# Sampling sets of twelve tokens, with the grid distances made in SBUF from turned rows

## The chip, the cores and the metric

The kernel runs on one core of one Trainium2 chip. The metric is the device time of one execution in microseconds (us), as a median of three runs. In the profile PE is TensorE's matmuls, PEld its weight loads, DVE VectorE, ACT ScalarE, POOL GpSimd, and SPq the queue of SyncE, which issues most transfers.

## The reference, cut to what matters

Four images of 32 x 32 tokens with 128 channels each pass three layers: a deformable convolution, an attention over slices, and a mixture of eight experts. Only the sampling of the first layer changes here. Per token, with 8 groups (g) of 32 channels and 9 points (k) each:

```python
px = ww + deform[..., 0];  py = hh + deform[..., 1]
x0 = jnp.floor(px);  y0 = jnp.floor(py)
wx1 = px - x0;  wx0 = 1.0 - wx1
wy1 = py - y0;  wy0 = 1.0 - wy1
samp = gather(y0, x0) * (wy0 * wx0)[..., None] + gather(y0, x0 + 1) * (wy0 * wx1)[..., None] \
     + gather(y0 + 1, x0) * (wy1 * wx0)[..., None] + gather(y0 + 1, x0 + 1) * (wy1 * wx1)[..., None]
out = jnp.einsum('bhwgkc,bhwgk->bhwgc', samp, weights)
```

`gather` takes the value of one pixel of the group, and zero outside the image. All of it is float32.

## The kernel before, in words

**The sampling as products.** The kernel gathers nothing. The weight of pixel (y, x) for a point at (py, px) is max(0, 1 - |y - py|) * max(0, 1 - |x - px|), so one token of a group has a 32 x 32 matrix A[y, x], the sum over its nine points of an outer product, and its output is A times the group's values (`vd`). An image has 8 groups, the program 32 (`IMAGES_GROUPS`, `ig` in the code).

**Sets.** A set is what one pair of 64-row halves of TensorE's array does at once. Before, it is 8 tokens: two halves (`NI`) of `NU * NV` = 4 tokens, 36 of 64 rows. `ysb` is the stationary operand (u by 32 rows y = 64 columns), `xsb` the moving one (32 columns x by v = 64). A group has 128 sets in four batches of 32; each batch is built and used in two halves of 16 sets, so there are eight halves, called slots here, per group and 256 in the program.

**One slot** (`k = 2 * n + pair`) passes these stations: `distances` on TensorE (L770: two bf16 matmuls whose stationary operand `lp` holds the positions split in three bf16 parts, and whose moving operand `spread_b` gives each set its 32 grid points; they leave p - q in PSUM banks 4 and 5); ACT `take_x` (L1170) and `x_ramps` (L1180, two instructions) make `xsb`; DVE `take_y` (L1475) clamps the y distance into `yr`, and POOL multiplies it with the rows `rw` into `ysb` (L691, two instructions); TensorE `products` (L783, 32 matmuls, seen as 64 in the trace since each float32 one is two passes) writes one of two pairs of PSUM banks; DVE `take` (L1485) copies them to `asb`. `distances` and `take_y` run three slots ahead of the products.

**One group** ends with `contract` (L798: 128 matmuls of A with `vd`, PSUM banks 0 to 3), ACT `spread_out` (L1187), and a group later `project` (L806) and DVE `conv_add` (L1494).

**What sets the order.** Each engine has one instruction stream, written out by loops over the slots; semaphores (`s.a_summed` and so on) join them. Into each slot `side` puts pieces of other work from tables of slot numbers: the preparation of the next images' positions (`PE_PREP`, `DVE_PREP`, ...; slots of image 0 only), and for the image before, attention (slots 2 to 33), sorting tokens by expert (30 to 42), and one expert tile per slot (`TILE_SLOTS`, L1023 and L1036, two lots of 4 matmuls). After the last group a tail runs the last image's side work alone. The preparation (`find_places`, `split_places`, `edge_weights`, L1415 to L1457 on DVE) leaves the positions as bf16 parts and the weights as float32 rows; both go to DRAM and come back by DMA, group by group.

## Time and profile before

| | us |
|---|---|
| median of 3 runs (1462.43 to 1470.79) | 1466.11 |
| span of the profiled execution | 1426.0 |
| median less span (launch and end lie outside the span) | 40.1 |
| before the first product | 63.0 |
| the 32 groups, to the last product | 1149 |
| the tail | 214 |
| busy: PE, PEld | 1075.1, 864.2 |
| busy: DVE, ACT, POOL | 877.5, 755.4, 700.6 |

The profile was taken of one execution and gives no time of it beyond its span. Busy times are sums over an engine's own instructions; they overlap between engines. Two things are to be kept in mind when reading: the trace lacks about half the records of the bf16 matmuls (259 of 512, while their 512 weight loads are all there), and the ends of matmuls are modelled, so that the starts of TensorE's instructions are the firmer numbers.

### The profile page before, as it was taken

How to read it: one execution, taken by the hardware profiler on the slowest of the kernel's cores; microseconds unless marked ns; L12 is line 12 of the kernel's file. 1: busy time of each engine (PE TensorE's matmuls, PEld its weight loads, DVE VectorE, ACT ScalarE, POOL GpSimd, SP SyncE). 2: the span in 40 equal slices, each digit the busy share in tenths (PEclk: the TensorE clock that was granted, in tenths of full speed). 3: DMA queues.
4: the chain of work that ended last, by engine and by line, in shares of the span. 5: the costliest groups of instructions: out<-in, count | busy, mean ns of one | idle time of the engine just before them, and what ended most of it. 6: DMA issues, size and time to landing. Idle time of an engine off the chain costs nothing.

```text
span 1426.0 us, 63149 instructions
## 1 busy us (share of the span) xinstructions
PE 1075.1 (75%) x27983; PEld 864.2 (61%) x28236; DVE 877.5 (62%) x1579; ACT 755.4 (53%) x1444; POOL 700.6 (49%) x675
## 2 busy tenths in 40 slices
PE   3477777876886789988877789988767899785290
PEld 2365655664575568875656578865655688544290
DVE  6577768776767765566776655567886654345311
ACT  2456667665564556765643566665554565221060
POOL 6365556664442854448536644467438543211304
PEclk9689899999998899999987899999988999965595
DMA  6513141421000435521113225511013254101761
GB/s 151 146 30 63 52 104 51 109 92 35 27 28 19 115 83 160 160 79 49 33 34 104 81 82 163 146 52 45 12 49 118 71 163 141 44 15 36 228 193 57
DMA packets 166290, 121.97 MB, mean 86 GB/s; under 512 B 45642, under 2 KB 146051, under 8 KB 165507
## 3 DMA queue, kind: packets, MB, share of 16 engines
q1 hardware_dynamic: 161922, 109.53, 27.3%
q0 software_dynamic: 4096, 8.40, 2.0%
q8 instruction: 223, 3.65, 1.1%
q14 instruction: 49, 0.39, 0.1%
HBM read 89.38 MB, written 28.51 MB: 83 GB/s over the span
## 4 chain that ended last, share of the span: by engine, by line
PE 36%; DVE 16%; issue 7%; ACT 3%; POOL 3%; DMA 1%; another core or an unknown queue 1%; POOLq 0%; DVEq 0%; ACTq 0%
PE ps L798 9%; PE ps L783 6%; PE ps L1023 6%; PE ps L1036 5%; PE ps L806 3%; DVE asb L1485 3%; DVE yr L1475 2%; PE ps L770 2%; DVE region L1711 2%; DVE x_tok L1727 1%; POOL sorted_rows L660 1%; PE ps L929 1%; POOL ysb L691 1%; PE ps L928 1%; PE ps L982 1%
## 5 line engine op out<-in xcount | busy, mean ns | idle before, releaser
L691 POOL TENSOR_TENSOR ysb<-yr,rw 128x512 f32<-128x512 f32 x512 | 551.5, 1101 | 494.1 <-DVE yr L1475 440.6
L1485 DVE COPY asb<-ps 128x1024 f32<-128x1024 f32 x256 | 311.7, 1218 | 91.2 <-PE ps L783 89.7
L1180 ACT ACTIVATE xsb<-xr,pick 128x512 f32<-128x512 f32 x512 | 362.7, 768 | 3.4
L783 PEld LDWEIGHTS ps<-xsb,ysb 64*64 64x64 f32 x16384 | 283.6, 142 | 94.5 <-issue 68.0
L783 PE MATMUL ps<-xsb,ysb 64*64 64x64 f32 x16384 | 321.2, 230 | 18.5 <-issue 8.4
L1475 DVE TENSOR_SCALAR yr<-ps 128x512 f32<-128x512 f32 x256 | 174.3, 681 | 205.9 <-PE ps L770 199.5
L798 PE MATMUL ps<-asb,vd 32*32 32x256 f32 x8192 | 190.8, 406 | 43.5 <-DVE asb L1485 24.1
L1170 ACT ACTIVATE xr<-ps 128x512 f32<-128x512 f32 x256 | 152.2, 595 | 99.3 <-remote 98.7
L770 PE MATMUL ps<-spread_b,lp 128*128 128x512 bf16 x259 | 103.6, 402 | 118.3 <-DVE yr L1475 65.8
L798 PEld LDWEIGHTS ps<-asb,vd 32*32 32x32 f32 x8192 | 127.8, 106 | 95.5 <-issue 65.1
L1187 ACT ACTIVATE osp<-ps 128x256 f32<-128x256 f32 x128 | 39.8, 405 | 273.8 <-PE ps L798 273.8
L1253 ACT ACTIVATE region<-ps,b_col 128x128 f32<-128x128 f32 x368 | 105.1, 373 | 79.4 <-PE ps L1023 79.4
L670 POOL DMA_INDIRECT picked<-expert_rows,row_no x64 | 61.6, 963 | 112.5 <-DMA expert_rows<-region 95.6
L660 POOL DMA_INDIRECT sorted_rows<-region,row_no x64 | 63.5, 992 | 107.4 <-DVE row_no L1676 92.0
L770 PEld LDWEIGHTS ps<-spread_b,lp 128*128 128x128 bf16 x512 | 34.1, 98 | 114.4 <-DVE yr L1475 63.4
L1023 PEld LDWEIGHTS ps<-region,ring 128*128 128x128 f32 x616 | 80.6, 194 | 10.3 <-issue 1.8
L1023 PE MATMUL ps<-region,ring 128*128 128x128 f32 x616 | 82.5, 278 | 0.9 <-ACT region L1253 0.9
L1036 PE MATMUL ps<-ring,region 128*128 128x128 f32 x616 | 81.6, 275 | 0.9 <-DVE region L1717 0.5
L806 PE MATMUL ps<-outw,osp 128*128 128x128 f32 x512 | 71.4, 297 | 11.1 <-DVE x_tok L1616 5.1
L1036 PEld LDWEIGHTS ps<-ring,region 128*128 128x128 f32 x616 | 75.0, 192 | 1.5 <-ACT region L1253 1.2
L806 PEld LDWEIGHTS ps<-outw,osp 128*128 128x128 f32 x512 | 65.8, 208 | 14.7 <-DVE x_tok L1616 5.5
L1717 DVE COPY region<-ps 128x128 f32<-128x128 f32 x92 | 26.7, 291 | 74.2 <-PE ps L1036 74.2
(236 smaller groups left out, 1087.1 us busy)
## 6 DMA issues: line engine op xcount, KB each, us to landing
ring<-in_L_ffn_W SPq DMA_DIRECT2D x154, 256.0 KB, 3.2
vd<-group_values SPq DMA_DIRECT2D x128, 128.0 KB, 2.7
asb<-in_L_ffn_W SPq DMA_DIRECT2D x30, 256.0 KB, 4.2
lp<-position_parts SPq DMA_DIRECT2D x96, 64.0 KB, 2.9
position_parts<-ring SPq DMA_DIRECT2D x3, 1536.0 KB, 6.2
group_values<-region SPq DMA_DIRECT2D x32, 128.0 KB, 3.4
weight_rows<-picked SPq DMA_DIRECT2D x4, 1024.0 KB, 4.3
rw<-weight_rows SPq DMA_DIRECT2D x32, 128.0 KB, 2.6
```

Source lines behind the costliest of these rows:

```text
L691: pl.tensor_tensor(ysb[:, n % 2, pair * CHUNK:(pair + 1) * CHUNK, u, :], yr[:, k % 3, :, :], rw[:, ig % 2, u, first:first + CHUNK].rearran ...
L770: pe.matmul(ps[:, bank, :], lp[:, ig % 2, beta, d, :], spread_b[:, half * CHUNK:(half + 1) * CHUNK, :].rearrange("p s q -> p (s q)"), star ...
L783: last = pe.matmul(o[:, :, NV * q:NV * q + NV], ysb[rows, n % 2, col, :, :].rearrange("p u y -> p (u y)"), xsb[rows, n % 2, col, :, :], st ...
L798: last = pe.matmul(ps[32 * jc:32 * jc + 32, j, 0:256], vd[rows, ig % 2, x, :], asb[rows, x, :, :, :].rearrange("p i n m -> p (i n m)"), st ...
L806: last = pe.matmul(pcol(project_bank(ig), t), osp[:, t, :], outw[:, ig % G, :], start=True, stop=True)
L1023: last = pe.matmul(ps[:, hidden_bank(b, i), j * P:(j + 1) * P], ring_part(r, 0)[:, j * P:(j + 1) * P], xsT[:, i, :], start=True, stop=True)
L1036: last = pe.matmul(ps[:, expert_bank(b, i), 0:C], hT[:, i % 2, j, :], ring_part(r, 1)[:, j * P:(j + 1) * P], start=(j == 0), stop=(j == HJ ...
L1170: act.activation(xr[:, half * CHUNK:(half + 1) * CHUNK, :].rearrange("p s q -> p (s q)"), ps[:, X_BANK, :], ACT.Relu, bias=1.0, scale=-1.0 ...
L1180: act.activation(xsb[:, n % 2, sets, :, v], xr[:, sets, :], ACT.Relu, bias=pick[:, v:v + 1], scale=-1.0).then_inc(s.x_ready, 1)
L1253: last = act.activation(hT[:, i % 2, j, :], ps[:, hidden_bank(b, i), j * P:(j + 1) * P], ACT.Gelu, bias=b1_col[:, i, j:j + 1])
L1475: dve.tensor_scalar(yr[:, k % 3, :, :].rearrange("p s q -> p (s q)"), ps[:, Y_BANK, :], 0.0, 1.0, ALU.max, ALU.min).then_inc(s.y_taken, 1)
L1485: dve.tensor_copy(asb[:, :, :, 2 * beta + pair, :].rearrange("p x i m -> p i x m"), ps[:, 2 * pair:2 * pair + 2, :].rearrange("p i (x m) - ...
```

## The change

**Sets** have twelve tokens: `NV` is 3, so a half holds 6 tokens and 54 of 64 rows, the moving operand has 96 columns, and a group has 86 sets (1032 token places for 1024 tokens). They are built in three chunks of 30, 28 and 28 sets; each chunk's products are made in three passes of 5 or 4 pairs of sets. So a group has nine slots (288 in all), an image 72, and the tables of side work are moved to match: tiles stand in slots 45 to 68, most attention steps one slot later.

**Distances.** `distances`, the bf16 parts, `spread_b`, `lp` and their transfers are gone. Positions are turned by TensorE together with the weights into rows of 86 sets (`rowstage`, then `rw`); DVE subtracts the grid from the x positions in SBUF (`x_distances`), POOL from the y positions (`y_distances`). ACT makes the three x ramps of a chunk in place in `xsb`; DVE clamps y in SBUF (`y_ramp`). The first two groups read `rowstage` itself and wait for no transfer.

**PSUM.** Banks 4 and 5 are free of distances and become the first of three pairs of product banks. `contract` now stands after the next group's first side work, ahead of its first products.

**Preparation** works on 86 partitions with 12 tiles of tokens where there were 8 on 128, so each of its DVE instructions over positions has half as many elements again; the splitting into parts is gone.

The diff, cut to its core:

```diff
-NI, NA = 2, 4
-NU, NV = 2, 2
+NI, NU, NV = 2, 2, 3
+NA = NU * NV
...
-BATCHES, SETS = 4, 32
+SETS = 86
+CHUNK_SETS = (30, 28, 28)
+PAIRS = ((5, 5, 5), (5, 5, 4), (5, 5, 4))
...
-GROUP_SLOTS = 2 * BATCHES
+GROUP_SLOTS = PARTS * len(CHUNK_SETS)
...
-TILE_SLOTS = tuple(range(44, 65)) + (66, 67, 68)
+TILE_SLOTS = tuple(range(45, 69))
...
-        X_BANK, Y_BANK = 4, 5
+        PRODUCT_BANK = (4, 0, 2)
...
+            def y_distances(ch):
+                ig, first, sets = chunk_of(ch)
+                if first == 0:
+                    wait_rows(pl, ig)
+                if ch >= 2:
+                    pl.wait_ge(s.y_ready, NU * (ch - 1))
+                pl.tensor_tensor(yr[:, ch % 2, 0:sets, :],
+                                 rows_of(ig)[:, 1, first:first + sets]...broadcast_to([P, sets, GRID]),
+                                 count[:, :]...broadcast_to([P, sets, GRID]),
+                                 ALU.subtract).then_inc(s.y_away, 1)
+            def weigh(ch):
+                pl.wait_ge(s.y_within, ch + 1)
+                if ch >= 2:
+                    pl.wait_ge(s.a_summed, PARTS * (ch - 1))
+                for u in range(NU):
+                    pl.tensor_tensor(ysb[:, ch % 2, 0:sets, u, :], yr[:, ch % 2, 0:sets, :], ...
+            for n in range(LAST):
+                ch, part_no = n // PARTS, n % PARTS
+                if part_no == 0:
+                    if ch + 2 < ALL_CHUNKS:
+                        y_distances(ch + 2)
+                    if ch + 1 < ALL_CHUNKS:
+                        weigh(ch + 1)
+                side(n // SLOTS, n % SLOTS)
...
-            def distances(k):
...
+                side(b, slot)
+                if at == 0 and ig:
+                    contract(ig - 1)
+                    if ig >= 2 and (ig - 1) % G:
+                        wait_for_banks(b, slot + 1)
+                        project(ig - 2)
...
+                if n % PARTS == 0:
+                    pe.wait_ge(s.x_ready, NV * (ch + 1))
+                    pe.wait_ge(s.y_ready, NU * (ch + 1))
+                if n >= 3:
+                    pe.wait_ge(s.a_taken, n - 2)
...
+            def x_edges(ch):
+                act.wait_ge(s.x_away, ch + 1)
+                away = xsb[:, ch % 2, 0:chunk_of(ch)[2], :, NV - 1]
+                act.activation(away, away, ACT.Relu, bias=1.0, scale=-1.0).then_inc(s.x_within, 1)
+            def x_ramp(ch, v):
+                act.activation(xsb[:, ch % 2, 0:sets, :, v], xsb[:, ch % 2, 0:sets, :, NV - 1], ACT.Relu,
+                               bias=pick[:, v:v + 1], scale=-1.0).then_inc(s.x_ready, 1)
...
-            def take_y(k):
+            def x_distances(ch):
+                if ch >= 2:
+                    dve.wait_ge(s.a_summed, PARTS * (ch - 1))
+                dve.tensor_tensor(xsb[:, ch % 2, 0:sets, :, NV - 1], rows_of(ig)[:, 0, ...], count..., ALU.subtract)
+            def y_ramp(ch):
+                dve.wait_ge(s.y_away, ch + 1)
+                v = yr[:, ch % 2, 0:sets, :].rearrange("p s q -> p (s q)")
+                dve.tensor_scalar(v, v, 0.0, 1.0, ALU.max, ALU.min).then_inc(s.y_within, 1)
...
             for n in range(LAST):
+                if n % PARTS == 0 and ch + 1 < ALL_CHUNKS:
+                    x_distances(ch + 1)
+                elif n % PARTS == 1 and ch + 2 < ALL_CHUNKS:
+                    y_ramp(ch + 2)
+                side(ig // G, n % SLOTS)
...
+                take(n)
```

On DVE, before, in slots of group 1 that also prepare image 1 (L1485 is the copy of the products, L1475 the clamp of a y distance, L1395 a step of the preparation):

```order
L1475 TENSOR_SCALAR yr<-ps 128x512 [waits y_ready,dy_summed]
L1395 TENSOR_TENSOR region<-ps,qbias 128x32x9 [waits columns_summed]
L1485 COPY asb<-ps 128x2x32x16 [waits a_summed]
L1475 TENSOR_SCALAR yr<-ps 128x512 [waits y_ready,dy_summed]
L1395 TENSOR_TENSOR region<-ps,qbias 128x32x9 [waits columns_summed]
L1485 COPY asb<-ps 128x2x32x16 [waits a_summed]
```

The same place on DVE after the change (L1490 is the copy, L1471 the x distances, L1482 the y clamp, L1411 the preparation):

```order
L1471 TENSOR_TENSOR xsb<-ring,count 128x896 [waits a_summed]
L1411 TENSOR_TENSOR region<-ps,qbias 86x32x9 [waits columns_summed]
L1490 COPY asb<-ps 128x2x32x15 [waits a_summed]
L1482 TENSOR_SCALAR yr<-yr 128x960 [waits y_away]
L1411 TENSOR_TENSOR region<-ps,qbias 86x32x9 [waits columns_summed]
L1490 COPY asb<-ps 128x2x32x15 [waits a_summed]
L1411 TENSOR_TENSOR region<-ps,qbias 86x32x9 [waits columns_summed]
L1490 COPY asb<-ps 128x2x32x12 [waits a_summed]
```

Instead of one clamp out of PSUM in each slot, DVE has per three slots one subtraction with two inputs in SBUF and one clamp from SBUF to SBUF; the second waits for POOL (`y_away`).

On PE, before, in the same slots (L770 the distances, L735 and L738 the preparation, L783 the products):

```order
L770 MATMUL ps<-spread_b,lp 128x512 [waits x_taken]
L770 MATMUL ps<-spread_b,lp 128x512 [waits y_taken]
L735 MATMUL ps<-wq,region 128x288 [waits columns_biased]
L738 MATMUL ps<-wv,region 128x256
L783 MATMUL ps<-xsb,ysb 64x32x2 [waits a_taken,y_ready,x_ready]
L783 MATMUL ps<-xsb,ysb 64x32x2 x31
```

And after (L764 and L745 the preparation, L793 the products), for the three passes of one chunk:

```order
L793 MATMUL ps<-xsb,ysb 64x32x3 [waits a_taken,y_ready,x_ready]
L793 MATMUL ps<-xsb,ysb 64x32x3 x19
L764 MATMUL ps<-wq,region 86x288 [waits values_copied,columns_biased]
L745 MATMUL ps<-wv,region 128x256
L793 MATMUL ps<-xsb,ysb 64x32x3 [waits a_taken]
L793 MATMUL ps<-xsb,ysb 64x32x3 x19
L764 MATMUL ps<-wq,region 86x288 [waits values_copied,columns_biased]
L745 MATMUL ps<-wv,region 128x256
L793 MATMUL ps<-xsb,ysb 64x32x3 [waits a_taken]
L793 MATMUL ps<-xsb,ysb 64x32x3 x15
```

The two distance matmuls and their waits are gone from every slot, and the products wait for `x_ready` and `y_ready` once per chunk instead of once per slot.

On POOL, after, from group 1 on (L671 the y distances, L684 the weighing; before there were only pairs of L691 of 16 sets each):

```order
L671 TENSOR_TENSOR yr<-rw,count 128x896 [waits y_ready]
L684 TENSOR_TENSOR ysb<-yr,rw 128x30x32 [waits a_summed,y_within]
L684 TENSOR_TENSOR ysb<-yr,rw 128x30x32
L671 TENSOR_TENSOR yr<-rw,count 128x896 [waits y_ready]
L684 TENSOR_TENSOR ysb<-yr,rw 128x28x32 [waits a_summed,y_within]
L684 TENSOR_TENSOR ysb<-yr,rw 128x28x32
```

POOL has three longer instructions per chunk where it had two short ones per slot.

## Rows read from the trace of the kernel before

**Rows 1.** Windows: the three loops of images 0 to 2, then the last (busy us by engine).

```profile
63.00:328.00 265.00, 201.84 (x6501) 158.11 (x6564) 190.57 (x241) 172.67 (x281) 157.07 (x132) 0.92 0.26 71
328.00:624.00 296.00, 243.68 (x7018) 198.56 (x7087) 192.59 (x339) 176.48 (x343) 151.32 (x147) 0.96 0.29 81
620.00:923.00 303.00, 249.57 (x6933) 204.21 (x6997) 198.75 (x354) 173.73 (x343) 164.09 (x161) 0.93 0.30 84
923.00:1212.00 289.00, 239.89 (x6644) 195.03 (x6703) 193.86 (x349) 166.88 (x327) 157.45 (x154) 0.94 0.28 81
```

**Rows 2.** Timeline, PE in expert slots with distances: start, duration, engine, line, operation.

```profile
562.44 1.16 PE L783 MATMUL ps<-xsb,ysb 64*64 64x64 f32 x64
565.85 1.16 PE L783 MATMUL ps<-xsb,ysb 64*64 64x64 f32 x64
```

**Rows 3.** Timeline, PE in the last expert slots of the loop, where no distances are left.

```profile
1201.48 1.16 PE L783 MATMUL ps<-xsb,ysb 64*64 64x64 f32 x64
1204.56 1.16 PE L783 MATMUL ps<-xsb,ysb 64*64 64x64 f32 x64
```

**Rows 4.** Page, part 5: groups by line (busy us, mean ns | idle before).

```profile
L691 POOL TENSOR_TENSOR ysb<-yr,rw 128x512 f32<-128x512 f32 x512 | 551.5, 1101 | 494.1 <-DVE yr L1475 440.6
L1485 DVE COPY asb<-ps 128x1024 f32<-128x1024 f32 x256 | 311.7, 1218 | 91.2 <-PE ps L783 89.7
L1180 ACT ACTIVATE xsb<-xr,pick 128x512 f32<-128x512 f32 x512 | 362.7, 768 | 3.4
L783 PE MATMUL ps<-xsb,ysb 64*64 64x64 f32 x16384 | 321.2, 230 | 18.5 <-issue 8.4
L1475 DVE TENSOR_SCALAR yr<-ps 128x512 f32<-128x512 f32 x256 | 174.3, 681 | 205.9 <-PE ps L770 199.5
L798 PE MATMUL ps<-asb,vd 32*32 32x256 f32 x8192 | 190.8, 406 | 43.5 <-DVE asb L1485 24.1
L1170 ACT ACTIVATE xr<-ps 128x512 f32<-128x512 f32 x256 | 152.2, 595 | 99.3 <-remote 98.7
```

**Rows 5.** Waits: who waited for whom (us in total, times, longest us).

```profile
PE ps L770 <- DVE yr L1475: 65.8, 57, 4.0
PE ps L798 <- DVE asb L1485: 24.1, 10, 4.8
PE ps L770 <- ACT xr L1170: 11.0, 11, 1.9
```

**Rows 6.** Single lines on DVE and POOL: durations in ns, min/median/max.

```profile
L1421 DVE TENSOR_TENSOR region<-region,pos x8: 746/756/1601, 36.5 to 278.7; 128x576 f32<-128x576 f32 x8
L1376 DVE TENSOR_TENSOR ring<-region x4: 1175/1180/1184, 20.0 to 233.5; 128x992 f32<-128x992 f32 x4
L1430 DVE TENSOR_SCALAR region<-region x8: 448/456/1303, 38.0 to 282.4; 128x576 f32<-128x576 f32 x8
L691 POOL TENSOR_TENSOR ysb<-yr,rw x512: 1036/1048/2167, 60.5 to 1202.2; 128x512 f32<-128x512 f32 x171
```

**Rows 7.** Timeline, before the first products: a column step, position work, the last edge weights.

```profile
29.74 0.65 PE L735 MATMUL ps<-wq,region 128*128 128x288 f32 x2
35.10 1.36 DVE L1415 SCALAR_TENSOR_TENSOR region<-region 128x1152 f32<-128x1152 f32 x1 [1.95 <-ACT region L1133]
40.90 0.96 DVE L1457 SCALAR_TENSOR_TENSOR region<-region 128x144 f32<-128x144 f32 x4
55.71 0.63 PE L770 MATMUL ps<-spread_b,lp 128*128 128x512 bf16 x1 [8.68 <-DMA lp<-position_parts]
63.04 1.73 PE L783 MATMUL ps<-xsb,ysb 64*64 64x64 f32 x64
```

**Rows 8.** Timeline, two preparation slots on PE: weight loads of the products.

```profile
101.01 1.02 PEld L783 LDWEIGHTS ps<-xsb,ysb 64*64 64x64 f32 x64 [0.33 <-issue]
103.56 1.02 PEld L783 LDWEIGHTS ps<-xsb,ysb 64*64 64x64 f32 x64 [0.33 <-issue]
```

**Rows 9.** Timeline, PE in the tail: two of image 2's last expert tiles.

```profile
1224.62 1.06 PE L1023 MATMUL ps<-region,ring 128*128 128x128 f32 x8
1226.99 1.13 PE L1023 MATMUL ps<-region,ring 128*128 128x128 f32 x8 [0.43 <-ACT region L1253]
```

653 lines of the change are left out of this document (310 added, 343 removed), and 8 rows, old and new, of the table DVE_STEPS.

## Prediction

> **What bounds the kernel now.** I read the windows by image first. In the loop PE is busy 76 to 83% of the time, DVE 65 to 72%, ACT 57 to 65%, POOL 51 to 59% [rows 1]. No engine is full, but PE is nearest, and its records of the distances are half missing, so it is nearer than the share says. Then the timeline of slots with an expert tile, the densest ones. Products start at 562.44 and again at 565.85: 3.41 us a slot, with PE idle for hardly anything [rows 2]. So there PE itself sets the pace. In slots with attention or preparation the pace comes from chains through PE, DVE and ACT: PE waited 65.8 us for DVE's clamp and 11.0 us for ACT ahead of its distances [rows 5], while POOL waited 440.6 us for the same clamp [rows 4]. That says that POOL is far from being a bound and that the y path of a slot (distances, clamp, weighing) is a chain of short links.
>
> **What leaves PE.** The last slots of the loop have no distances left, and there the slot takes 1204.56 - 1201.48 = 3.08 us [rows 3] against 3.41 [rows 2]. So a slot's two distance matmuls, with the change of tile shape around them, cost 0.33 us on a PE that is full: 256 x 0.33 = 84 us. The waits of 65.8 + 11.0 = 77 us stood ahead of them and go too, but the chains that fed them stay in another form, so the range of that term is 0 to -77, and I take half, -38.
>
> **The products.** A pass of 32 matmuls with 64 columns takes 1.16 us [rows 2]. If time goes by instructions, 172 matmuls per group for 256 take a third off 321.2 us [rows 4], -105. If it goes by columns, 172 x 96 = 16,512 against 256 x 64 = 16,384 per group, no change. A matmul of 256 columns shows 406 ns and one of 64 shows 230 [rows 4], so the duration follows the columns, and I take 0. There are 32 passes more (288 for 256), each with a start like the 0.33 us ahead of a pass [rows 8]: +10. PE by itself: -84 + 10 = -74.
>
> **DVE's own work.** Removed: 256 clamps, 174.3 us. Added: 96 subtractions of 896 or 960 elements with both inputs in SBUF. The nearest rows are 746 ns for 576 elements and 1180 for 992 [rows 6], which is 1.04 ns an element and 0.15 us a start, so 1.08 us each, 104 us. And 96 clamps in SBUF: 448 ns for 576 elements [rows 6]; up to 448 x 896 / 576 = 0.70 us each, 60 to 67 us. The copies of the products: 288 for 256, of 7 x 960 + 2 x 768 elements a group, against 8 x 1024: the same elements and 32 more starts of 0.15, +5 us. Sum 104 + 64 + 5 - 174 = about 0. Preparation gains and loses a few us per image (longer instructions, no parts): 0.
>
> **POOL's own work.** Three instructions per chunk for two per slot. 512 elements take 1.048 us [rows 6]; by elements 896 take 1.83, and 96 x 3 of them (some of 960) 537 us against 512 x 1.048 = 537: no change. If a part of the 1.048 is fixed it is less; nothing shows it to be more. **ACT**: 4 instructions of 896 elements per chunk for 6 or 9 of 512. With 768 ns for 512 [rows 4], between 0.77 us (all of it fixed) and 1.34 (in proportion): 295 to 515 us against 362.7 + 152.2 = 515. A gain or nothing, beside other work; the cover if it is nothing is that ACT is busy 60% [rows 1].
>
> **What DVE and POOL do to each other.** This is the term that decides. A DVE subtraction over SBUF takes 746 ns at best and 1601 at worst, the clamp form 448 and 1303, always about 0.85 us more, and POOL's own instruction goes from 1036 to 2167 ns [rows 6]. The copies out of PSUM have no such tail: DVE's L1475 has a mean of 681. So a DVE instruction that works in SBUF waits for a running POOL instruction to end, and the other way round. Before, the two hot DVE instructions read PSUM and were free of it. Now 96 x 2 = 192 more DVE instructions have it, and POOL's instructions last 1.83 us instead of 1.05. POOL is busy about 55% of the loop; a wait is half an instruction on average, 0.9 us: 192 x 0.55 x 0.9 = +95 us of DVE time. The side work's waits grow too. Medians of 756 and 456 near the minimum, beside maxima 0.85 above it, say that a minority is hit; I take 70 instructions of the loop's side work at 0.85 us, 60 us (an estimate), and 60 x (1.83 / 1.05 - 1) = +45. DVE then is occupied 140 us more, 191 + 193 + 199 + 194 + 140 = 917 of some 1080 [rows 1]: it becomes as full as PE. How much of the 140 reaches the end? Between 0 (all in DVE's idle time, of which there were 1149 - 777 = 372 us) and 140; at such a share a third is my choice: +47.
>
> The Trainium skill, SBUF — State Buffer, section "Who interferes with whom", says that a VectorE instruction with two SBUF inputs, or in a two-port mode, and a GpSimd instruction that reads SBUF exclude each other for their whole length, whoever comes first. The trace agrees (746 against 1601, 448 against 1303). By that rule a group's POOL work and the two new DVE forms add up on one port, which is the third rival below.
>
> **Ends of a group.** PE waited 24.1 us for the last copies ahead of `contract` [rows 5]; now side work stands between. But where there is none, `project` no longer covers that wait. I take -5 (range -25 to +20).
>
> **Before the first products.** From the last edge weights (40.90 + 0.96 = 41.9) to the first products (63.0) lie casts, a store and loads; PE waited 8.68 us for a load alone [rows 7]. Now the rows are used where ACT leaves them. Four more column products of 0.65 us and position work half as long again (L1415 from 1.36 to 2.0, five others like it) put 41.9 back by about 5; then turning and copying about 3 (a guess between 2 and 4), POOL's two distances and first weighing 4 x 1.83 = 7.3: 57. So -6 (0 to -10). **Tail**: three tiles of image 2, one each 1226.99 - 1224.62 = 2.4 us [rows 9], leave the tail, where they stand ahead of the last image's first steps: -5 of these 7.
>
> **Sum.** -74 - 38 + 47 - 5 - 6 - 5 = -81 on the profiled span of 1426.0, so 1345. The span lies 40.1 us under the median of the runs; that part doesn't change. 1466.1 - 81 = 1385.
>
> **The rivals.**
> - PE was the bound throughout and nothing new comes: the whole 77 us of waits go and the port costs nothing in the end. 1466 - 74 - 77 - 5 - 11 = 1299. For it: POOL and ACT have slack and all is built a chunk ahead, with three product buffers. Against: two engines above 80% that must wait for each other in fixed order seldom overlap so well. Chance 0.13.
> - The port sets the pace where side work is thin. A group needs 86 x 3 x 32 elements on POOL, 16.8 us, and DVE adds 3 x (1.08 + 0.65) = 5.2: 22 us or 2.4 us a slot, almost what a preparation slot took before (103.56 - 101.01 = 2.55 [rows 8]), and there are now nine. A tile slot loses the 0.33 and, with 1920 columns for 2048, 0.07 more. Image 0's 265 us and the thin groups gain nothing; what is left is 72 tile slots x 0.40 = 29 us, and 11 at the ends: 1426. By the rule quoted above this is what a port shared between the two would do. For it: DVE was 72% busy in image 0, the most of all [rows 1]. Chance 0.20.
> - Slower. DVE meets POOL at every chunk, by construction: the same semaphore (`a_summed`) releases POOL's weighing and the copy after which DVE's subtraction stands, so it arrives in the middle of the first weighing each time, and the clamp in the next. Were each of the 192 to wait a full 1.83 us, DVE would need 777 + 351 + 45 = 1173 us in a loop that took 1149: +24 with no idle at all, +86 with a twentieth of idle (1235). Less the 11 at the ends, between 1479 and 1541; I price it at 1510. It decides from a mean wait of about 1.1 us per instruction, where 777 + 211 + 45 = 1033 is 90% of the loop. Chance 0.13.
> - The change does as it says, and all cancels: within 0.5%, 7.3 us, about what can be told from no change. Chance 0.04.
>
> **How the numbers follow.** My forecast, 1340 to 1425 around 1385, has 0.50; the first rival 0.13, the port as pace 0.20, slower 0.13, nothing 0.04. The range of 8 in 10 goes from 1300 (which leaves out half of the first rival) to 1455 (which leaves out the slower case). The terms' own ends, -74 - 77 - 25 - 10 - 5 = -191 and -74 + 140 + 20 - 5 = +81, lie beyond it. Faster by over 0.5%: 0.50 + 0.13 + 0.19 = 0.82; the same 0.05; slower 0.13.
>
> **What would show it.** In the profile after: no L770, and tile slots with products 3.0 us apart (right for PE); the subtraction's minimum near 1.08 us and its mean near 1.6, 1.08 + 0.55 x 0.9 (right for the port); above 2.2 the slower case holds. POOL's mean near 1.9 to 2.2 us. The clamp's minimum at 0.6 to 0.7. First products at 57. A pass of 20 matmuls with 96 columns at about 1.1 us; if it is 0.8, the products went by instructions. What would make me wrong: PE waiting for `x_ready` at each chunk, since copy, subtraction and four ACT instructions in a row are 1.2 + 1.1 + 4 x 1.1 = 6.7 us after a chunk's end, which a thin chunk of three passes does not cover.

## The result and the profile after

The changed kernel takes 1587.88 us (median of 4 runs, 1583.44 to 1590.45), the kernel before 1464.27 on the same chips (4 runs, 1458.64 to 1470.79): ratio 1.0842, 95% interval 1.0799 to 1.0885. I had forecast 1385 with a range up to 1455. So the sign was wrong, by some 200 us. The profiled execution took 1589.51 us with a span of 1587.5. Here and in every later run the time lies only 2 us above the span. The profile of before has a span of 1426.0, 38 us under its median, and no time of its own. By the same 2 us its execution would have taken 1428 us, where the quickest of some 70 timed ones took 1452.64. So differences between its rows and those of the later traces are too large by some 35 us over the whole span; where in the span they lie is not known. Times and ratios do not have this fault.

The windows of [rows 1], the loops of images 0 to 2 and the last one, and then the tail (us; busy time of PE, PEld, DVE, ACT, POOL; granted clock; DMA share; GB/s).

```profile
54.00:364.00 310.00, 205.38 (x5165) 162.84 (x5164) 227.68 (x237) 189.55 (x187) 164.95 (x76) 0.80 0.19 48
364.00:688.00 324.00, 250.77 (x5526) 201.62 (x5525) 211.47 (x330) 199.14 (x248) 169.96 (x94) 0.85 0.25 72
688.00:1030.60 342.60, 259.30 (x5529) 205.98 (x5528) 223.34 (x346) 197.74 (x246) 181.25 (x104) 0.84 0.24 70
1030.60:1349.60 319.00, 236.46 (x5255) 190.48 (x5254) 215.26 (x341) 188.29 (x237) 158.87 (x91) 0.87 0.24 70
1349.60:1587.50 237.90, 129.61 (x889) 95.84 (x885) 68.55 (x238) 48.14 (x122) 45.56 (x48) 0.66 0.28 82
```

An image takes 310 to 343 us for 265 to 303 [rows 1], and the last stretch 238 for 214. PE is busy for as long as before (205, 251, 259 against 202, 244, 250), though a fifth of its instructions is gone: its granted clock is 0.80 to 0.87 for 0.92 to 0.96. The same clock over a whole execution is 0.811 to 0.818 in the four runs of the changed kernel and 0.885 to 0.904 in all but one of before. And PE's idle time has grown by 42, 21 and 30 us an image. The groups of the page that answer to [rows 4]:

```profile
L684 POOL TENSOR_TENSOR ysb<-yr,rw 128x960 f32<-128x960 f32 (+1 forms) x180 | 384.4, 2157 | 524.9 <-PE ps L793 519.5
L1177 ACT ACTIVATE xsb<-xsb,pick 128x896 f32<-128x896 f32 (+1 forms) x288 | 434.7, 1565 | 2.1
L1490 DVE COPY asb<-ps 128x960 f32<-128x960 f32 (+1 forms) x288 | 317.6, 1107 | 98.0 <-PE ps L793 76.8
L793 PE MATMUL ps<-xsb,ysb 64*64 64x96 f32 x11008 | 333.0, 273 | 40.0 <-ACT xsb L1177 22.0
L808 PE MATMUL ps<-asb,vd 32*32 32x258 f32 x8192 | 232.0, 462 | 81.6 <-DVE asb L1490 61.8
L1171 ACT ACTIVATE xsb<-xsb 128x896 f32<-128x896 f32 (+1 forms) x96 | 147.8, 1540 | 226.4 <-DVE xsb L1471 225.9
L671 POOL TENSOR_TENSOR yr<-rw,count 128x896 f32<-128x896 f32 (+1 forms) x90 | 179.7, 1997 | 14.7 <-DMA rw<-set_rows 7.3
L1471 DVE TENSOR_TENSOR xsb<-rw,count 128x896 f32<-128x896 f32 (+1 forms) x90 | 179.2, 1991 | 0.0
L1482 DVE TENSOR_SCALAR yr<-yr 128x896 f32<-128x896 f32 (+1 forms) x96 | 85.3, 889 | 3.4 <-POOL yr L671 3.4
```

The subtraction takes 1.99 us in the mean, ACT's four instructions of a chunk 1.54 to 1.57 each (582 us in all, for 515 before), and the contraction (`L808`) 232 us for 191. ACT waited 226 us for the subtraction.

Three places show how that reaches PE. First, expert slots, PE's timeline and then ACT's (start, duration, engine, line); `L793` are the products, `L1037` and `L1050` the expert's matmuls.

```profile
570.77 1.05 PE L793 MATMUL ps<-xsb,ysb 64*64 64x96 f32 x40
573.74 1.06 PE L793 MATMUL ps<-xsb,ysb 64*64 64x96 f32 x40
580.05 1.06 PE L793 MATMUL ps<-xsb,ysb 64*64 64x96 f32 x40
582.21 1.13 PE L1037 MATMUL ps<-region,ring 128*128 128x128 f32 x8 [1.10 <-ACT region L1252]
584.16 0.89 PE L793 MATMUL ps<-xsb,ysb 64*64 64x96 f32 x32
```

```profile
579.48 1.57 ACT L1177 ACTIVATE xsb<-xsb,pick 128x896 f32<-128x896 f32 x1
580.94 1.13 ACT L1252 ACTIVATE region<-ps,b_col 128x128 f32<-128x128 f32 x4
```

A slot without a wait is 573.74 - 570.77 = 2.97 us, the 3.0 that I had forecast for the slots of [rows 2]. But the one from 580.05 to 584.16 is 4.1: ACT's Gelu (`L1252`) stands behind a ramp of 1.57 us, and PE waits 1.10 us for it. Of the 60 expert slots that have no contraction in them 24 take 2.97 us, 18 take 3.3 to 3.4, and 18 take 3.8 to 4.1; before, 51 of 58 took 3.41. The mean is 3.4 us now and 3.5 before.

Second, a chunk's start in an image's attention, all engines:

```profile
487.73 4.92 DVE L1607 TENSOR_SCALAR region<-region,norms 128x128 f32<-128x128 f32 x8
488.10 3.45 POOL L684 TENSOR_TENSOR ysb<-yr,rw 128x896 f32<-128x896 f32 x2 [8.95 <-PE ps L793]
495.47 0.70 PE L993 MATMUL ps<-marks,earlier 128*128 128x72 f32 x2 [7.56 <-DVE gate L1656]
496.41 1.34 DVE L1471 TENSOR_TENSOR xsb<-rw,count 128x896 f32<-128x896 f32 x1
497.78 1.42 ACT L1171 ACTIVATE xsb<-xsb 128x896 f32<-128x896 f32 x1 [7.90 <-DVE xsb L1471]
```

Eight instructions of DVE that take 0.333 us each at their shortest take 4.92 us together, for 2.7: POOL starts two weighings 0.4 us behind the first. With POOL's instructions short (below) the slowest of these takes 0.346 us, here 1.732. PE waits 7.56 us at the end of that chain.

The contraction at the turn of image 1 to 2 shows a third thing (PE and POOL; then windows of 1 us of `L808` alone, with the number of its matmuls behind the busy time of PE):

```profile
671.37 6.78 PE L808 MATMUL ps<-asb,vd 32*32 32x258 f32 x109
673.22 1.01 POOL L653 DMA_INDIRECT picked<-expert_rows,row_no  x1 [0.15 <-POOL ysb L684]
...
680.41 0.65 PE L808 MATMUL ps<-asb,vd 32*32 32x258 f32 x5 [0.81 <-issue]
681.84 3.20 PE L808 MATMUL ps<-asb,vd 32*32 32x258 f32 x70 [0.78 <-issue]
```

```profile
672.00:673.00 1.00, 1.00 (x56) 0.89 (x34) 0.50 0.06 16
676.00:677.00 1.00, 0.88 (x9) 0.32 (x10) 1.00 0.24 66
```

From 673 to 681 POOL issues six indirect loads of `picked` in a row. From 675 on PE gets through 4 to 11 matmuls per microsecond, for some 50 just before, waiting for no semaphore ("issue"). This contraction lasts 15.9 us, the next such 15.9, the last of all 24.2, all others 5.3 to 8.1.

### The profile page after: what moved, and what is told of

It reads as the page before. It is cut to its first block, busy times and chain, and to the rows that moved or that the text cites. A ratio compares the mean times of both kernels' runs of the same rounds, so it can differ in the third digit from the quotient of the medians.

```text
span 1587.5 us, 50101 instructions
## 1 busy us (share of the span) xinstructions
PE 1103.0 (69%) x22444; PEld 874.2 (55%) x22444; DVE 979.3 (62%) x1555; ACT 842.2 (53%) x1059; POOL 738.0 (46%) x448
## 4 chain that ended last, share of the span: by engine, by line
PE 43%; DVE 28%; ACT 12%; issue 10%; POOL 4%; SPq 1%; DMA 1%; another core or an unknown queue 1%; POOLq 0%; DVEq 0%; ACTq 0%
PE ps L808 14%; DVE asb L1490 6%; ACT xsb L1177 5%; PE ps L793 5%; PE ps L1037 4%; PE ps L816 4%; DVE xsb L1471 4%; PE ps L1050 3%; ACT region L1252 3%; POOL picked L653 2%; DVE yr L1482 2%; DVE region L1715 2%; DVE x_tok L1499 2%; PE ps L764 1%; DVE x_tok L1731 1%
## 5 line engine op out<-in xcount | busy, mean ns | idle before, releaser
L684 POOL TENSOR_TENSOR ysb<-yr,rw 128x960 f32<-128x960 f32 (+1 forms) x180 | 384.4, 2157 | 524.9 <-PE ps L793 519.5
L1177 ACT ACTIVATE xsb<-xsb,pick 128x896 f32<-128x896 f32 (+1 forms) x288 | 434.7, 1565 | 2.1
L1490 DVE COPY asb<-ps 128x960 f32<-128x960 f32 (+1 forms) x288 | 317.6, 1107 | 98.0 <-PE ps L793 76.8
L793 PE MATMUL ps<-xsb,ysb 64*64 64x96 f32 x11008 | 333.0, 273 | 40.0 <-ACT xsb L1177 22.0
L793 PEld LDWEIGHTS ps<-xsb,ysb 64*64 64x64 f32 x11008 | 283.7, 152 | 100.0 <-issue 48.2
L808 PE MATMUL ps<-asb,vd 32*32 32x258 f32 x8192 | 232.0, 462 | 81.6 <-DVE asb L1490 61.8
L1171 ACT ACTIVATE xsb<-xsb 128x896 f32<-128x896 f32 (+1 forms) x96 | 147.8, 1540 | 226.4 <-DVE xsb L1471 225.9
L808 PEld LDWEIGHTS ps<-asb,vd 32*32 32x32 f32 x8192 | 154.6, 114 | 151.9 <-issue 124.5
L671 POOL TENSOR_TENSOR yr<-rw,count 128x896 f32<-128x896 f32 (+1 forms) x90 | 179.7, 1997 | 14.7 <-DMA rw<-set_rows 7.3
L1471 DVE TENSOR_TENSOR xsb<-rw,count 128x896 f32<-128x896 f32 (+1 forms) x90 | 179.2, 1991 | 0.0
L1252 ACT ACTIVATE region<-ps,b_col 128x128 f32<-128x128 f32 x368 | 105.0, 372 | 92.0 <-PE ps L1037 91.9
L1186 ACT ACTIVATE osp<-ps 128x258 f32<-128x258 f32 x128 | 42.9, 442 | 170.5 <-PE ps L808 170.5
L1037 PE MATMUL ps<-region,ring 128*128 128x128 f32 x616 | 89.6, 290 | 32.2 <-ACT region L1252 27.6
L1037 PEld LDWEIGHTS ps<-region,ring 128*128 128x128 f32 x616 | 77.0, 197 | 42.6 <-issue 35.1
L1482 DVE TENSOR_SCALAR yr<-yr 128x896 f32<-128x896 f32 (+1 forms) x96 | 85.3, 889 | 3.4 <-POOL yr L671 3.4
L1050 PE MATMUL ps<-ring,region 128*128 128x128 f32 x616 | 81.7, 275 | 3.0 <-ACT region L1252 3.0
L1050 PEld LDWEIGHTS ps<-ring,region 128*128 128x128 f32 x616 | 75.0, 192 | 3.6 <-ACT region L1252 3.6
```

What stands on the lines that cost most here:

```text
L671: pl.tensor_tensor(yr[:, ch % 2, 0:sets, :], rows_of(ig)[:, 1, first:first + sets].rearrange("p (s o) -> p s o", o=1) .broadcast_to([P, se ...
L684: pl.tensor_tensor(ysb[:, ch % 2, 0:sets, u, :], yr[:, ch % 2, 0:sets, :], rows_of(ig)[:, 2 + u, first:first + sets].rearrange("p (s o) -> ...
L793: last = pe.matmul(o[:, :, NV * q:NV * q + NV], ysb[rows, ch % 2, col, :, :].rearrange("p u y -> p (u y)"), xsb[rows, ch % 2, col, :, :], ...
L808: last = pe.matmul(ps[32 * jc:32 * jc + 32, j, 0:NI * AM], vd[rows, ig % 2, x, :], asb[rows, x, :, :].rearrange("p i n -> p (i n)"), start ...
L1037: last = pe.matmul(ps[:, hidden_bank(b, i), j * P:(j + 1) * P], ring_part(r, 0)[:, j * P:(j + 1) * P], xsT[:, i, :], start=True, stop=True)
L1050: last = pe.matmul(ps[:, expert_bank(b, i), 0:C], hT[:, i % 2, j, :], ring_part(r, 1)[:, j * P:(j + 1) * P], start=(j == 0), stop=(j == HJ ...
```

## The experiments

Below, "gain" is the difference of two ratios to the kernel before, times 1464 us; before ran beside every kernel. The intervals of the ratios reach 0.3 to 0.8 points to each side (4 to 12 us). A gain over the changed kernel has that kernel's 0.4 points in it too, which makes it sure to 8 to 11 us (an estimate, the two taken as independent). So gains of 11 and 16 us are just told from nothing, the one of 10 us is not, and none of them is told from the others.

### Where the time went

**Indirect loads away from the contraction** (`pick_rows`, GpSimd):

```diff
                     pl.wait_ge(s.expert_stored, 16 * 3 * (b + 1))
+                    pl.wait_ge(s.out_summed, min(G * (b + 2), IMAGES_GROUPS))
```

> GpSimd waits for the end of the contraction before it issues the indirect loads of `picked`; nothing else changes. Theory 'place': the 8.4% come in part from the picks, which by the new slot numbers start just when `contract` of a group starts. In the changed kernel the three contractions that meet them last 15.9, 15.9 and 24.2 us, all others 5.3 to 8.1. If the picks slow TensorE down, these three go to 6 to 8 us and the kernel to 1588 - 9 - 9 - 17 = 1553, give or take 10. Rival 'port' and rival 'x chain': the contraction's matmuls don't use what GpSimd uses, they were slow for another reason (a lower clock, late copies); contractions stay at 16 and 24 us and the time within 5 us of 1588, or above it, since the picks are now later.

Measured 1566.85 us, ratio 1.0731 (1.0665 to 1.0796): a gain of 16 us. The three contractions fell to 7.5, 7.7 and 6.6 us, so the loads were the cause. But in the loop the loss only moved on: groups 15 to 17 (counted from 0) take 33.6, 52.1 and 54.7 us for 43.4, 43.5 and 51.2, so what was gained is the 17.6 us of the last contraction. The timeline of this kernel behind the contraction:

```profile
676.21 1.00 POOL L654 DMA_INDIRECT picked<-expert_rows,row_no  x1 [4.43 <-PE ps L809]
678.71 0.66 PE L794 MATMUL ps<-xsb,ysb 64*64 64x96 f32 x7 [0.18 <-issue]
...
681.87 0.41 PE L794 MATMUL ps<-xsb,ysb 64*64 64x96 f32 x4 [1.02 <-issue]
```

Now it is a pass of 40 products that dribbles, from 678.7 to 685.6 where 1.05 us would do.

**Ramps laid out contiguous** (`xsb` with v outside, x inside):

```diff
-        xsb = sb("xsb", [P, 2, CHUNK, GRID, NV])
+        xsb = sb("xsb", [P, 2, CHUNK, NV, GRID])
-                                             xsb[rows, ch % 2, col, :, :], start=True, stop=True,
+                                             xsb[rows, ch % 2, col, :, :].rearrange("p v x -> p x v"), start=...
```

> The three ramps of x are laid out one behind the other (v outside, x inside), so that ScalarE's four instructions and VectorE's subtraction read and write rows of 32 neighbours instead of every third element; TensorE reads its moving operand with a stride instead. Theory 'x chain': ScalarE's 1.54 to 1.57 us per 896 elements and the subtraction's minimum of 1.34 come from the stride; they go to about 1.1 and 1.08, the chain of a chunk from 9.4 us to 6.6, and the time by 20 to 60 us to between 1528 and 1568. Rival 'port' and rival 'place': ScalarE was not the bound (53% busy), time within 10 us of 1588. If TensorE pays for its strided reads, the pass of 40 matmuls goes above 1.06 us and the time up.

Measured 1563.90 us, ratio 1.0697 (1.0649 to 1.0745): a gain of 21 us, in spite of PE. The page, and a pass in an expert slot:

```profile
L793 PE MATMUL ps<-xsb,ysb 64*64 64x96 f32 x11008 | 393.7, 295 | 20.7 <-issue 9.4
L1177 ACT ACTIVATE xsb<-xsb,pick 128x896 f32<-128x896 f32 (+1 forms) x288 | 290.7, 1059 | 2.1
L1171 ACT ACTIVATE xsb<-xsb 128x896 f32<-128x896 f32 (+1 forms) x96 | 93.0, 969 | 279.6 <-DVE xsb L1471 279.5
```

```profile
1305.09 1.35 PE L793 MATMUL ps<-xsb,ysb 64*64 64x96 f32 x40
```

ACT's four fell from 582 to 384 us. Every third element had cost it half as much again. PE paid for the stride instead: 1.35 us a pass for 1.05.

**GpSimd's instructions short** (the same line in `y_distances` and `weigh`), and **ramps short** (`x_ramp`, and the same in `x_edges`):

```diff
+                sets = sets if ch < 4 else 2
-                sets = chunk_of(ch)[2]
+                sets = chunk_of(ch)[2] if ch < 4 else 2
```

> GpSimd's subtraction and two weighings treat 2 sets instead of 28 or 30 from the fifth chunk on (this part of the computation is left out; all waits stay). It takes some 700 us of GpSimd's work away, and with it nearly every meeting of VectorE and GpSimd. Theory 'port': VectorE's subtraction falls from a mean of 1.99 us to 1.35, its clamp from 0.89 to 0.62, its side work too; that is 90 us of VectorE's time and as much again of the side work, and 60 to 120 us of the end: 1470 to 1530. Rival 'x chain' and rival 'place': 0 to 25 us, 1563 or more, since GpSimd itself was never waited for (PE waits 1.8 us for it) and the chain of copy, subtraction and ScalarE stays at 8 us.

Measured 1504.10 us, ratio 1.0269 (1.0216 to 1.0321): a gain of 84 us, the largest of all single ones. The subtraction and the clamp in this kernel (min/median/max in ns):

```profile
L1473 DVE TENSOR_TENSOR xsb<-rw,count x90: 1331/1402/1635, 107.5 to 1257.7; 128x896 f32<-128x896 f32 x60, 128x960 f32<-128x960 f32 x30
L1484 DVE TENSOR_SCALAR yr<-yr x96: 607/618/2140, 46.3 to 1251.4; 128x896 f32<-128x896 f32 x64, 128x960 f32<-128x960 f32 x32
```

DVE's busy time fell from 979 to 851 us. Copies, subtractions and clamps make 73 of that; the other 55 is side work (all of DVE less those three groups: 397 us, now 343) that no longer meets POOL. Two things keep the 84 us from being the price of what the change added. Before, POOL had 551 us of such work too, and the side work took 877.5 - 311.7 - 174.3 = 391 us, hardly less than now; no run took POOL's work out of that kernel. And with POOL early, its indirect loads (those of `sorted_rows` too) fall on six contractions of 12.1 to 24.4 us instead of three.

> ScalarE's four instructions of a chunk treat 2 sets instead of 28 or 30 from the fifth chunk on (this part of the computation is left out; all waits and the subtraction stay). 582 us of ScalarE's work go down to about 90. Theory 'x chain': the wait of the products at a chunk's start goes, as do the late expert steps behind 1.5 us of ramps (tile slots of 4.1 and 3.8 us go to 3.0); time down by 50 to 100 us, 1490 to 1540. Rival 'port': VectorE is the bound, ScalarE's time was hidden: 1570 or more. Rival 'place': the same, 1575 or more.

Measured 1546.81 us, ratio 1.0589 (1.0531 to 1.0646): a gain of 37 us. Of the 60 expert slots 45 now take 2.97 us and none of the others over 3.4, and a group of nine takes 35 us for 39. Each rival named in these two had its own share; none was the whole.

**Loads and additions eight slots later:**

```diff
-PICK_SLOT, PICK_SLOTS = 72, 8
-ADD_SLOT = 80
+PICK_SLOT, PICK_SLOTS = 80, 8
+ADD_SLOT = 88
```

> The indirect loads of `picked` and the additions of the rows (VectorE) are moved from slots 72 to 79 and 80 to 87 to 80 to 87 and 88 to 95. With 72 slots an image that puts them beside the same steps of the next image as before the change (slots 8 to 15 and 16 to 23 of it), away from slot 0 with its contraction and from VectorE's heaviest attention steps (9 to 17). Theory 'place': the groups 16, 17, 24 and 25 of the changed kernel last 43.5, 51.2, 43.2 and 51.1 us against 36.8, 36.7, 36.4 and 36.9 before; they lose 5 to 12 us each, the contractions of 16 and 24 us go to 7, and the time falls by 30 to 60 us, 1528 to 1558, more than the 21 us of the run in which the picks only waited for the contraction. Rival 'port and ramps are all there is': the adds cost VectorE the same wherever they stand, so not more than those 21 us, 1565 or more.

Measured 1568.62 us, ratio 1.0775 (1.0710 to 1.0839): a gain of 10 us, not told from nothing. The contractions of groups 15 and 23 fell to 7.5 us; the last one, in the tail, kept 24.7. Groups 16 and 17 stayed at 44.8 and 51.3 us, and group 18 went from 41.6 to 44.0. But the run did not do what it was made for. The loads met the next contraction instead, that of groups 16 and 24, which takes 13.9 us for 6.9 and 6.5:

```profile
707.23 7.51 PE L808 MATMUL ps<-asb,vd 32*32 32x258 f32 x181
712.44 0.94 POOL L653 DMA_INDIRECT picked<-expert_rows,row_no  x1 [0.30 <-issue]
```

So the 30 to 60 us did not come, and whether the steps that the additions stand beside matter is left open.

**Three at once** (GpSimd short, ramps short, slots eight later):

> GpSimd short, ramps short (both leave their part of the computation out) and the picks eight slots later, in one kernel. If the three causes are separate and complete, the gains add: 84 + 41 + 30 to 60, so 1588 falls to 1403 to 1433, and little is left above my forecast of 1385 (which had 47 us of the port in it, so 1338 without). If they share one path (each only waits for the next), the sum is smaller: 1440 to 1480. If it stays at 1460 or more, something fourth holds the kernel, such as the order of chunks or TensorE's clock.

Measured 1459.11 us, ratio 0.9986 (0.9959 to 1.0013): a gain of 125 us, against 84 + 37 + 10 = 131 for the three alone. So they add up within the noise (some 20 us for such a sum). The 125 us are as much as the slowdown, but they do not account for it. The two short edits also take away work that the kernel before has too. And the loads are not gone: with POOL early six contractions have 6 to 16 indirect loads in them. Five of these last 11.1 to 15.3 us and the last one 27.3, together some 56 us above the 6.6 us of the others, where the changed kernel has 36 (estimates). One of the six:

```profile
468.86 7.17 PE L810 MATMUL ps<-asb,vd 32*32 32x258 f32 x108 [5.37 <-DVE asb L1492]
474.59 0.96 POOL L643 DMA_INDIRECT sorted_rows<-region,row_no  x1 [0.30 <-issue]
```

My forecast without the port was 1385 - 47 = 1338, 121 us less. These loads can be 56 of that; the rest is a gain that I had counted on and that did not come.

### The gain that was not there

**The kernel before, its distances cut to a sixteenth of their columns:**

```diff
-                    pe.matmul(ps[:, bank, :], lp[:, ig % 2, beta, d, :], ...
+                    sets = CHUNK if k < 2 else 1
+                    pe.matmul(ps[:, bank, 0:GRID * sets], lp[:, ig % 2, beta, d, :], ...
```

> The kernel before, its distance matmuls cut from 16 sets (512 columns) to 1 (32 columns) from the third pass on (this part of the computation is left out; clamps, copies and waits stay). It prices by itself what I let leave TensorE. Theory of the prediction: 84 us of pace and part of 77 us of waits; with weights and waits still there, 256 x 0.25 us: 1462 down to 1380 to 1410. Rival: TensorE's time was not what set the pace outside the tile slots; only 72 to 96 tile slots gain 0.3 us each, 20 to 30 us: 1430 to 1445. At 1450 or more the whole term was an illusion.

Measured 1449.27 us, ratio 0.9924 (0.9893 to 0.9954): 11 us, where I had 84. Expert slots did fall from 3.41 to 3.12 us, which is 72 x 0.29 = 21 us. Outside them nothing was gained. The mean granted clock fell too: 0.835 to 0.846 in the six executions, for 0.888 to 0.903 in the fifteen of the kernel before beside them. Group 17 before and the same group in this kernel show what that looks like (the window columns as above, then PE's timeline):

```profile
656.70:693.40 36.70, 30.98 (x828) 20.23 (x832) 27.31 (x30) 21.13 (x35) 26.89 (x27) 1.00 0.20 55
```

```profile
659.90:706.70 46.80, 41.82 (x836) 27.03 (x832) 27.71 (x30) 21.72 (x36) 27.09 (x28) 0.74 0.15 43
```

```profile
677.45 1.16 PE L783 MATMUL ps<-xsb,ysb 64*64 64x64 f32 x64
679.02 1.12 PE L928 MATMUL ps<-region,ws_bd 128*128 128x512 f32 x2
```

```profile
687.11 1.99 PE L784 MATMUL ps<-xsb,ysb 64*64 64x64 f32 x64
689.10 2.06 PE L929 MATMUL ps<-region,ws_bd 128*128 128x512 f32 x2
```

In these two executions PE is busy for longer with less to do, 41.8 us for 31.0: the granted clock is 0.74 for 1.00, and the same instructions take 1.99 us for 1.16 and 2.06 for 1.12, which is the lower of the clock's two levels. Six groups (9, 11, 17, 19, 25, 27) are 38 us longer together than in the trace of before. But that cannot be laid to the edit: the two traces are 34 us apart the wrong way, for a kernel that is 11 us faster, and this execution (1461.59 us) is the slowest of its six. In the changed kernel group 17 has a clock of 0.77 and lasts 51.2 us. The Trainium skill, TensorE: Matmul & The Clock Gate, section "HAM oscillation — how this bites in real kernels", describes a kernel in which waits between short matmul stretches put the clock down again and again; here the runs agree as far as that less work between the same waits lowered the mean clock, 0.84 for 0.90.

**Work given back to TensorE**, two bf16 matmuls without use in each slot that has no expert tile, in the changed kernel:

```diff
+            def keep_busy(n):
+                if n < 3 or (n >= SLOTS and tile_of(n % SLOTS)):
+                    return
+                pe.wait_ge(s.a_taken, n - 2)
+                for i in range(2):
+                    pe.matmul(ps[:, PRODUCT_BANK[n % PARTS] + i, :]..., ident..., ones..., start=True, stop=True)
```

> The changed kernel with two more bf16 matmuls of 512 columns in every slot without an expert tile, into the bank that the slot's products start anew: work as the distances were, with no result that anyone reads. Theory 'clock': the change took that work from TensorE where it was not full, and the granted clock fell (groups 16 to 20: 0.80, 0.77, 0.80, 0.74, 0.78 against 0.95, 1.00, 0.91, 0.79, 0.85 before), so that attention steps took up to twice as long (the distance run on the kernel before: a pair of steps of 1.10 us took 2.07). With the work back the clock of these groups returns to 0.9 or more, group 17 goes from 51 us to 41 to 45, and although TensorE has some 60 us more to do the kernel is 10 to 50 us faster: 1538 to 1578. Rival 'the clock is a consequence': the clock follows from the waits and costs nothing itself; the extra matmuls then cost 20 to 60 us: 1605 or more.

Measured 1611.13 us, ratio 1.0976 (1.0918 to 1.1034): 20 us slower. The mean clock went from 0.811 to 0.846 only.

> The same extra matmuls, with the contiguous ramps and the picks behind the contraction. Each is a repair of a cost found so far, nothing is left out. If they add (24 + 21 + the clock's 10 to 50), 1490 to 1530; it would still not beat the kernel before, because the 84 us of the port are left. If the extra matmuls cost, 1550 to 1600.

Measured 1568.83 us, ratio 1.0690 (1.0640 to 1.0740), clock 0.866: no better than the contiguous ramps alone (1.0697), though the loads are moved in it too.

The mirror, in the kernel before, each distance matmul issued twice where there is no expert tile:

```diff
+                    again = 2 if k >= 3 and (slot < SLOTS or not tile_of(slot % SLOTS)) else 1
+                    for _ in range(again):
```

> The kernel before with each distance matmul issued twice in slots without an expert tile: 368 more matmuls of 0.21 us. It is the mirror of the run that shortened them. Theory 'clock': before had groups at 0.79, 0.85 and 0.91; they rise, which pays for the added 77 us wholly or in part: between 15 us faster and 10 us slower, 1445 to 1470, with the mean clock above 0.92 for 0.897. Rival 'TensorE's work is on the path': +40 to +77 us, 1500 to 1537.

Measured 1484.17 us, ratio 1.0134 (1.0101 to 1.0168): 20 us slower for 77 us of work, mean clock 0.908 to 0.915. Its group 17:

```profile
682.70:727.10 44.40, 39.34 (x844) 25.05 (x848) 27.78 (x30) 21.31 (x34) 26.99 (x27) 0.92 0.16 42
```

> GpSimd short, ramps short, picks eight slots later (as in the run of three at once, 1459 us), with the extra matmuls. If the clock is the fourth cause beside these three, 1459 falls by 20 to 60 us, to 1400 to 1440, near the 1385 that I forecast. If it is not, it rises by 20 to 60 us.

Measured 1471.76 us, ratio 1.0043 (1.0011 to 1.0074): 8 us slower than without.

So of 84 us that PE is relieved of 11 are kept, and adding work does not pay for itself, whatever it does for the clock. "The clock is the fourth cause, beside the three" is refuted as something to repair. How much of the missing 73 us the lower clock takes back, and how much was never to be had because PE waits in those slots, is not separated. Group 17 ran at 1.00 with the distances, 0.74 with a sixteenth and 0.92 with the double. It is longer than before in both (46.8 and 44.4 us for 36.7), with less work and with more, as are groups 16, 24 and 25, so the trace of before is probably an unusually good one just there.

### How the port and the loads work

**VectorE without instructions at the port** (on the contiguous ramps: the subtraction as the same instruction on `pl`, the clamp on `act`):

```diff
+                act.activation(v, v, ACT.Relu, bias=1.0, scale=-1.0).then_inc(s.y_halved, 1)
+                act.wait_ge(s.y_halved, ch + 1)
+                act.activation(v, v, ACT.Relu, bias=1.0, scale=-1.0).then_inc(s.y_within, 1)
```

> On top of the layout with the ramps one behind the other: the x subtraction goes to GpSimd, and the clamp of y to ScalarE as two Relu (1 - Relu(1 - d) in [0, 1]). VectorE then has no instruction of the products left but the copies out of PSUM. Theory 'port': VectorE loses 235 us, GpSimd gains 180 (to some 900), the meetings of the two are left to side work; by the 84 us that the short GpSimd instructions gave, 1564 falls to 1470 to 1520. Rival 'GpSimd becomes the bound': five instructions of 1.7 us a chunk are 27 us a group at least, with the indirect DMAs and the waits for side work above 30; at chunk starts TensorE waits for x_ready later than now: no gain or slower than 1564.

Measured 1566.38 us, ratio 1.0745 (1.0692 to 1.0797) against 1.0697: nothing gained. DVE's busy time fell to 770.5 us, of which the copies are 317.4, so side work takes 453 us for 402. POOL is busy for 808 us instead of 722; that it now meets the side work more would fit. ScalarE has two more instructions in the chain of y too, and this run does not separate the two.

**Each GpSimd instruction in two halves:**

```diff
+                    half = sets // 2
+                    for a in (0, half):
+                        last = pl.tensor_tensor(ysb[:, ch % 2, a:a + half, u, :], yr[:, ch % 2, a:a + half, :], ...
```

> Each of GpSimd's three instructions of a chunk is cut into two of 14 or 15 sets: the same elements, 288 starts of 0.2 us more (+60 us of GpSimd), half as long each. Theory 'port, whole instructions exclude each other': VectorE waits for the rest of a running GpSimd instruction, so its wait halves: the subtraction's mean falls from 1.99 us to 1.65 to 1.75, the side work's time by 20 to 30 us, the kernel by 15 to 40 us: 1548 to 1573. Rival 'GpSimd's total work is what counts' (its results come late, or any share of the port costs in proportion): the means stay, GpSimd has 60 us more to do, 1588 to 1605.

Measured 1576.92 us, ratio 1.0767 (1.0726 to 1.0807): a gain of 11 us, though POOL has more to do. Of this kernel:

```profile
L1478 DVE TENSOR_TENSOR xsb<-rw,count x90: 1339/1576/2302, 105.7 to 1332.4; 128x896 f32<-128x896 f32 x60, 128x960 f32<-128x960 f32 x30
```

The mean fell from 1.99 to 1.74 us, as forecast. The excess over the shortest went from 0.65 to 0.40: so the waits go with the length of one GpSimd instruction, not with the sum of its work.

**Loads between GpSimd's instructions, in pairs:**

```diff
+                side(n // SLOTS, n % SLOTS)
+                    weigh(ch + 1, lambda: side(n // SLOTS, n % SLOTS + 1))
+                side(n // SLOTS, n % SLOTS + 2)
```

> The indirect loads of a chunk's three slots are no longer issued six in a row behind the second weighing, but two behind the subtraction, two behind the first weighing and two behind the second. Slots, counts and everything else stay. Theory 'burst': six or more indirect loads in a row starve TensorE of instructions (40 products took 8 us for 1.1 under them, the contraction 15.9 for 6.5), pairs with 2 us between don't: contractions 16 and 24 of the loop go to 7 to 9 us and nothing is lost in the slots behind; 10 to 25 us faster, 1563 to 1578, with the tail's 24 us unchanged, since there the 16 still come in a row. Rival 'any indirect load slows TensorE': the same number, so the same loss spread wider: 1583 to 1593.

Measured 1561.77 us, ratio 1.0670 (1.0611 to 1.0729): a gain of 25 us, the most of the three ways to treat the loads. The two contractions take 11.5 us, not 7 to 9. So pairs slow PE too, only for less long; "burst" was right in sign, and the rival had a part. Contractions 11, 19 and 27, which meet the loads of `sorted_rows`, even grew, from 7.0, 7.4 and 8.1 us to 10.3, 9.9 and 9.9.

**All repairs together**, nothing left out (contiguous ramps, halves, pairs, and in the tail the loads behind the contraction):

> What the runs have found, together and with nothing left out: ramps contiguous (24 us by itself), GpSimd in halves, picks spaced, in the tail the picks behind the contraction (17 us of the 21). If these add: 1588 - 24 - 25 - 17 - 17 = 1505, range 1490 to 1530. It would not beat the kernel before.

Measured 1497.53 us, ratio 1.0221 (1.0175 to 1.0268): a gain of 91 us, where the parts by themselves gave 21 + 11 + 25 = 57 and the tail's contraction has 17 more to give: 74. The difference is within the noise of such a sum.

**The stride moved to TensorE's output:**

```diff
-                            last = pe.matmul(o[:, :, NV * q:NV * q + NV],
+                            last = pe.matmul(o[:, :, NV * q:NV * q + NV].rearrange("p x v -> p v x"),
-                                             xsb[rows, ch % 2, col, :, :].rearrange("p v x -> p x v"), ...
+                                             xsb[rows, ch % 2, col, :, :], ...
```

> The combined version, but TensorE now reads its moving operand contiguous too (v outside, x inside) and writes its columns in that order into a PSUM tile viewed the same way, so the stride is on its output. Theory: the strided read cost TensorE 0.3 us a pass (40 matmuls alone in 1.2 us instead of 0.9); a strided write costs nothing, as the products' tile was strided already. Passes back to 0.9 us, 1497 down by 15 to 50: 1447 to 1482. Rival: what slows TensorE is the jump between neighbours, wherever it is: no change, 1490 to 1505.

Measured 1466.41 us, ratio 1.0022 (0.9988 to 1.0056): a gain of 120 us over the changed kernel, 29 of them over the version with TensorE's strided reads, and level with the kernel before. Since nothing is left out here, the stride, the length of GpSimd's instructions and the loads are together enough to explain what the change lost. How much each took is known only roughly, from the single runs. Its ramps take what they took at the first change of layout, and a pass in an expert slot again what it took before:

```profile
541.67 1.06 PE L806 MATMUL ps<-xsb,ysb 64*64 64x96 f32 x40
```

**The clamp on ScalarE** (the lines shown above), and **side work ahead of subtraction and clamp**, both on that version:

```diff
+                side(ig // G, n % SLOTS)
                 if n % PARTS == 0 and ch + 1 < ALL_CHUNKS:
                     x_distances(ch + 1)
...
-                side(ig // G, n % SLOTS)
```

> As the run before this one, and the clamp of y goes from VectorE to ScalarE (two Relu of 0.97 us each; ScalarE was 41% busy). VectorE loses 89 us of instructions at GpSimd's port, GpSimd gains nothing. Theory 'port': 15 to 40 us faster than the run before this one. Rival: the run that also gave GpSimd the subtraction won nothing (1566 against 1564) because ScalarE's two instructions lengthen the chain of y: within 10 us of it, or slower.

Measured 1496.31 us, ratio 1.0224 (1.0141 to 1.0308): 30 us slower. POOL waits where it had hardly waited:

```profile
POOL ysb L691 <- ACT yr L1200: 126.2, 30, 10.8
```

> The repaired version with contiguous ramps (1466 us), and VectorE's subtraction and clamp stand behind the side work of their slot instead of ahead of it. Theory: in the slots with attention TensorE waits for VectorE's side step, and the subtraction (1.5 us) stands ahead of it although its chunk is two slots away; with it behind, the slots of 11 to 14 us at a chunk's start lose 1 to 2 us each, some 12 of them: 5 to 25 us faster than 1466, 1441 to 1461, which would be faster than the kernel before too. Rival: the chain of x (subtraction, four on ScalarE) is then late for the next chunk, or the subtraction only meets GpSimd elsewhere: 1460 to 1485.

Measured 1489.95 us, ratio 1.0215 (1.0177 to 1.0253): 28 us slower. ACT's wait for the subtraction went from the first row (the version before) to the second:

```profile
ACT xsb L1184 <- DVE xsb L1484: 231.5, 75, 8.7
```

```profile
ACT xsb L1184 <- DVE xsb L1484: 332.0, 91, 13.1
```

Both say the same: in this kernel one more link in either chain of a chunk cost 28 to 30 us, though the engine that took it had free time.

## Why the prediction was wrong

I had forecast a gain of 81 us, and 123 were lost, some 200 in all. Four steps failed: the relief of PE, the port, ScalarE, and the indirect loads.

- **What leaves PE, -84.** The step that failed most, by 73 us. The price per slot was right where PE is full (0.29 us for my 0.33 with the distances short, 2.97 us for 3.41 in a free slot of the changed kernel). It failed in that I multiplied it by all 256 slots. The distances by themselves are worth 11 us: about 21 in expert slots, and nothing in the others, where the mean clock is lower and PE waits for the other engines; which of the two it is stays open.
- **Waits ahead of the distances, -38.** Not separated by a run of its own. The run of the short distances keeps these waits, so it says nothing of them. In the changed kernel PE's other waits grew: for the last copies to 61.8 us from 24.1, for the Gelu to 27.6 from 0.9.
- **The products, 0.** Right: a pass of 40 records takes 1.05 us, the time follows the columns. All products take 333.0 us for 321.2, near the +10 that I gave to their starts.
- **DVE's own work, 0.** Wrong by 96 x 0.26 = 25 us of DVE's time. The subtraction's shortest is 1.34 us, not 1.08, as it writes every third element; written contiguous it is 1.08 (1081 ns in the repaired version). The clamp at 0.61 was right.
- **POOL's own work, 0.** Right: at its shortest 1.69 us for my 1.83, so slightly less than before [rows 6]; means 2.0 to 2.16.
- **ACT, gain or nothing.** Wrong in both halves. Its 582 us are outside my range of 295 to 515, since [rows 4] shows 0.77 us for a strided write with a contiguous read, and now both are strided. And "ACT is busy 60%, so it is covered" took a share of the whole for a statement on one slot; up to 37 us were on the path, by the run that takes nearly all of these instructions away. As what would make me wrong I had named the chain of copy, subtraction and four ACT instructions, with 4 x 1.1 us in it; it is 4 x 1.55. But I had PE waiting for `x_ready` at each chunk. It waited for that 9 times, 22.0 us in all; as much again (27.6 us, 33 times) it waited for the Gelu behind a ramp, which I had not thought of.
- **DVE and POOL, +47.** Right in mechanism; too small as it seems, but the size is known only between bounds. Without POOL's work the kernel is 84 us faster, but that takes away what the kernel before suffered too. The subtractions and clamps take 73 us less in that run, where I had +95; the side work 55 less, where I had 60 already before the change and +45 by it, and its time hardly rose (391 to 397 us). So the extra DVE time was rather 80 than 140, and it cost the end more than the third of it that I let through: a wait of DVE passes on to ACT and PE, as at 487.73. The mean wait of a subtraction is 0.65 us, below the 1.1 from which the third rival was to decide, so that rival, priced at 1510, gave the right sign by a mechanism that holds only in part: DVE is busy 65 to 73% of the loops, not all of them. The Trainium skill, SBUF — State Buffer, section "Who interferes with whom", was quoted for whole-instruction exclusion; the halves bear it out (0.65 to 0.40 us).
- **Ends of a group, -5, and tail, -5.** Missed altogether: the loads of `picked` start by slot number, at a group's first slot, as before. But before two of them met a contraction (6.3 us), since POOL did them slot by slot; now POOL is paced by chunks, so six come in a row on it. This I had put at nothing. The runs that treated them gave 10 to 25 us, and the one that gave 25 left the tail's contraction at 23.4 us. PE's wait for the last copies, 24.1 us in [rows 5], is 61.8 now.
- **Before the first products, -6.** Right: they start at 54.0 us for 63.0 [rows 7], -9.
- **The 40.1 us between span and median, which I said do not change.** They did: 0.4 us after (1587.88 - 1587.5). I took the profiled execution before for a typical one.

## What to carry to other kernels

An operation taken off the engine that is busiest was worth its time here only in the slots where that engine never waits; count those slots, and price the rest at nothing until a run with the operation cut short says otherwise. When a profile's span lies far under the timed runs, ask first whether that execution was like them. And when a run moves or shortens work, look where everything that it paced went: two runs here only moved the loads from one contraction to another. Three slots' work in one chunk does not only save starts: it lengthens every link of each chain and what an engine finds in front of it, and it bunches whatever else is paced by the chunk. Before a layout puts an operand at a stride, ask each engine that reads or writes it; here the only one that took one more for nothing was TensorE's write to PSUM.

## What the runs showed of the hardware

- Indirect loads issued by GpSimd slow TensorE's stream of short matmuls, both the products (40 in 7 us for 1.05) and the contraction (the last in 24.2 us for 6.6). It takes several: over all traces here a contraction without such loads takes 6.4 to 6.8 us in the mean, with two or three 5.6 to 9.1, with six 11.1 to 15.9, and with twelve to sixteen 23.4 to 27.6. In the changed kernel's DMA view from 1354 to 1372 us the queue that carries instructions moved one packet, the loads 416:

```profile
q0 software_dynamic: 416, 0.85, 18.2%
q8 instruction: 1, 0.02, 0.4%
```

  That PE lacks instructions there would fit, but no run shows it; what slows it is open.
- 896 fp32 elements on ScalarE take 0.97 to 1.06 us contiguous and 1.54 to 1.57 with every third one read and written. TensorE reading its moving operand with a step of 32 elements takes 1.35 us a pass for 1.05; writing single columns with a step of 12 or 15 elements into PSUM takes 1.06, no more than runs of three columns with that step. The Trainium skill, SBUF — State Buffer, section "Door 1: The DMA port swizzle", has it the other way round, fp32 free in SBUF up to a step of four elements and a matmul slowed by any pattern in PSUM that is not contiguous; for ScalarE and VectorE (1.34 us for 1.08 with a write of step 3) these rows decide otherwise. For PSUM they show only that single columns cost no more than runs of three; no run writes contiguous.
- TensorE's mean granted clock fell from 0.90 to 0.84 when work was taken from it (0.835 to 0.846 in six executions), and rose only from 0.81 to 0.85 when work was added to the changed kernel, which became 20 us slower by it.
